# A four-layer conditioned model on one core: the first chunk of three stages normalised in the stage ahead of each, L0's last LayerNorm moved into L1's Q/K/V stage, L1's weights loaded a stage ahead

## The reference

```
L0:  res = relu(concat([x, cumulative-value attention + cond]) @ ff1 + b1) @ ff2 + b2 + x
     x = (res - mean(res)) * rsqrt(var(res) + 1e-6) * gamma + beta            # LayerNorm
L1:  h = film(rmsnorm(x, w1), cond);  Q, K, V = h @ q_w + q_b, h @ k_w + k_b, h @ v_w + v_b
     x = x + softmax(Q K^T / 16) V @ proj_w + proj_b
     h = film(rmsnorm(x, w2), cond);  x = x + gelu(h @ mlp_w1 + b1) @ mlp_w2 + b2
L2:  h = gain(cond) * layernorm(x) + shift(cond);  qkv = h @ Wqkv^T + bqkv      # 16 heads of 16
     h1 = attention(qkv) @ Wp^T + bp + x;  x = h2(h1) + h1
L3:  LayerNorm, attention with 16 heads of 64, then 8 experts on 256 tokens each
```

## Time and profile before

| | |
|---|---|
| timed runs | median 2151.21 us of 3 (2143.28 to 2153.71) |
| profiled execution | 2135.19 us, span 2133.5 us |
| mean granted TensorE clock | 0.925 |
| TensorE busy | 1863.1 us, 87% |
| VectorE busy | 1479.1 us, 69% |
| ScalarE busy | 1186.0 us, 56% |
| GpSimd busy | 817.6 us, 38% |

### The profile page before, as it was taken

One profiled execution on the slowest core, in us unless ns is written; L12 is line 12 of the kernel. 1 busy time (PEld: TensorE's weight loads), 2 busy tenths in 40 slices (PEclk: granted clock), 3 DMA queues, 4 the chain that ended last, 5 costly groups with the idle time before them and its releaser, 6 DMA issues. The chain is left out here.

```text
span 2133.5 us, 37279 instructions
## 1 busy us (share of the span) xinstructions
PE 1863.1 (87%) x14338; PEld 1188.9 (56%) x14338; DVE 1479.1 (69%) x2497; ACT 1186.0 (56%) x2034; POOL 817.6 (38%) x735
## 2 busy tenths in 40 slices
PE   5888689879879999998788969999999999984796
PEld 3665467669533333333566745555555555583686
DVE  5554644363559998992788777777777777646796
ACT  2333233232206886885456667777777777632573
POOL 4355450074121212000155654544444444304376
PEclk8999899989878998999899989999999999996698
DMA  5000100000252312112156965444554565225452
GB/s 146 1 1 0 45 8 1 31 13 1 79 153 45 95 42 46 39 45 65 65 178 204 287 161 120 113 103 104 120 120 109 123 147 136 59 85 159 135 155 48
DMA packets 196273, 191.14 MB, mean 90 GB/s; under 512 B 64192, under 2 KB 154944, under 8 KB 195840
## 3 DMA queue, kind: packets, MB, share of 16 engines
q1 hardware_dynamic: 193024, 184.56, 32.4%
q0 software_dynamic: 3072, 4.20, 1.1%
HBM read 121.07 MB, written 67.37 MB: 88 GB/s over the span
## 5 line engine op out<-in xcount | busy, mean ns | idle before, releaser
L1470 POOL TENSOR_SCALAR l3h_prob<-l3h_prob,l3h_inv 128x1024 f32<-128x1024 f32 x256 | 287.5, 1123 | 322.0 <-DVE l3h_inv L1442 322.0
L1436 DVE TENSOR_REDUCE l3h_nmax<-l3h_score 128x1 f32<-128x1024 f32 x256 | 313.5, 1224 | 139.2 <-PE l3h_score L1379 139.1
L1660 DVE TENSOR_REDUCE l2h_nm<-l2h_rowb 128x1 f32<-128x1024 f32 x256 | 302.7, 1218 | 37.4 <-PE l2h_rowb L1591 37.0
L1695 ACT ACTIVATE l2h_pT<-l2h_score 128x512 f32<-128x512 f32 x512 | 274.6, 598 | 91.4 <-PE l2h_score L1613 68.3
L1460 ACT ACTIVATE l3h_prob<-l3h_score,l3h_nmax 128x1024 f32<-128x1024 f32 x256 | 285.9, 1117 | 38.5 <-DVE l3h_nmax L1436 3.4
L1402 PE MATMUL l3h_out<-l3h_pT,l3h_vs 128*64 128x512 f32 x1024 | 274.4, 617 | 0.0
L1428 ACT ACTIVATE l3h_pT<-l3h_ring 128x512 f32<-128x512 f32 x256 | 152.8, 597 | 105.2 <-PE l3h_ring L1390 104.7
L1390 PEld LDWEIGHTS l3h_ring<-ident,l3h_prob 64*128 64x128 f32 x4096 | 172.3, 139 | 37.3 <-issue 8.0
L1426 DVE COPY l3h_pT<-l3h_ring 128x512 f32<-128x512 f32 x256 | 172.1, 672 | 2.0 <-PE l3h_ring L1390 2.0
L1390 PE MATMUL l3h_ring<-ident,l3h_prob 64*128 64x64 f32 x4096 | 169.5, 222 | 2.6 <-DVE l3h_pT L1426 2.4
L1627 PE MATMUL l2h_out<-l2h_pT,l2h_vs 128*32 128x256 f32 (+1 forms) x1792 | 162.7, 437 | 0.0
(11 more groups left out here) (449 smaller groups left out, 4346.0 us busy)
## 6 DMA issues: line engine op xcount, KB each, us to landing
q3first<-l_q SPq DMA_DIRECT2D x64, 256.0 KB, 5.0
l3h_Q<-l_q SPq DMA_DIRECT2D x64, 256.0 KB, 5.0
l_q<-l3qkv_hi SPq DMA_DIRECT2D x16, 512.0 KB, 5.1
l_q<-l3qkv_lo SPq DMA_DIRECT2D x16, 512.0 KB, 4.0
l_k<-l3qkv_hi SPq DMA_DIRECT2D x16, 512.0 KB, 3.3
l_k<-l3qkv_lo SPq DMA_DIRECT2D x16, 512.0 KB, 3.4
k3first<-l_k SPq DMA_DIRECT2D x64, 128.0 KB, 5.2
l3h_vs<-l_v SPq DMA_DIRECT2D x32, 256.0 KB, 3.1
```

The source lines that it names most:

```text
L1436: dve.tensor_reduce(self.nmax[:, t % 4:t % 4 + 1], self.score[t % 2][:, :], AX.X, ALU.max, negate=True).then_inc(self.maxes, 1)
L1470: pool.tensor_scalar(self.prob[:, q, :], self.prob[:, q, :], self.inv[:, q:q + 1], self.vscale, ALU.mult, ALU.mult).then_inc(self.scaled, 1)
L1660: dve.tensor_reduce(self.nm[:, mr % 2, at:at + 1], self.rowb[h][:, :], AX.X, ALU.max, negate=True).then_inc(self.maxes, 1)
L1695: act.activation(self.pT[:, g % 4, h, c * C:(c + 1) * C], self.score[v % 3][:, :], ACT.Exp).then_inc(self.exps, 1)
```

## The change

- **State that outlives a stage.** `CarriedNorm`, a `NormTurn` for each of the three stages, lives in a buffer `carry` (128 x 4096 numbers) and has semaphores that aren't cleared between the stages. `carry` is L0's cumulative sum, and from its last use on it holds the normalised tiles of even chunks, the statistics, L1's weights, `oT`, the first quarters of the MLP's weights and what L2 needs.
- **L0**: no LayerNorm for chunk 3; the residual is written to `X`. Behind products 2 and 3 of chunk 3 VectorE makes the statistics of chunks 0 and 1 for L1, behind product 5 it normalises chunk 0. SP loads L1's three weight matrices and a copy of gamma and beta once the cumulative sum is dead.
- **L1's Q/K/V**: VectorE starts with chunk 1's normalisation, then does L0's LayerNorm of chunk 3 (gamma and beta too), with chunk 2's statistics within it; chunk 3's statistics come behind chunk 0's copies. TensorE no longer waits for loads. L2's weights aren't loaded here.
- **Attention**: VectorE makes the statistics of chunks 0 to 2 for the MLP behind the low parts of tiles 12, 13 and 14, and normalises chunk 0 behind those of tile 15; ScalarE takes three roots behind its last high part. SP loads half of the MLP's first weight matrix.
- **MLP**: starts with chunk 1's normalisation. VectorE instead of GpSimd makes the first two low weight parts, GpSimd begins when the first input is copied, and ScalarE rounds the last four quarters ahead of GELU 3 and 4. The statistics of chunks 0 to 2 for L2 and chunk 0's normalisation are made behind group 0 of chunks 2 and 3 and before the last residual. SP loads L2's weights.
- **L2's Q/K/V**: starts with chunk 1's normalisation and chunk 3's statistics.

The core of the diff (signatures, views and semaphore lists left out):

```diff
@@ layer0: sync, scalar, vector; the pool's last finish(NC - 1) is removed
+            sp.wait_ge(clo, NC * KF)
+            for n in ("qw", "kw", "vw"):
+                sp.dma_start(g[f"l1_{n}"], w1[n].rearrange("(k p) n -> p k n", p=P)).then_inc(ahead, 16)
+            for n in ("gam", "bet"):
+                sp.dma_start(g[f"l0_{n}"], w[n].rearrange("(a n) -> a n", a=1).broadcast_to([P, D])).then_inc(ahead, 16)
+            sp.wait_ge(ahead, 16 * 5)
...
+                    if c == NC - 1 and j == 4:
+                        nt.act_root(act, 0)
+                        nt.act_root(act, 1)
...
+                    if c == NC - 1 and j in (2, 3):
+                        dve.wait_ge(shifted, (j - 1) * TC)
+                        nt.dve_stats(dve, j - 2)
+                    if c == NC - 1 and j == 5:
+                        nt.dve_norm(dve, 0)
...
+                    to = X if c == NC - 1 else res
+                if c == NC - 1:
+                    break
@@ layer1_qkv: scalar, tensor, vector
-            nt.act_start(act)
-            act.wait_ge(loaded, 96)
+            nt.act_scale(act, 0)
+            act.wait_ge(inverse0, 1)
+            act.activation(rstd[:, :], rstd[:, :], ACT.Sqrt).then_inc(root0, 1)
+            nt.act_root(act, 2)
+            act.wait_ge(loaded, 48)
...
-            pe.wait_ge(loaded, 96)
...
-            nt.dve_start(dve)
+            last = T - TC
+            nt.dve_norm(dve, 1)
+            for i in range(TC):
+                dve.bn_stats(st[:, i, :], X[:, last + i, :]).then_inc(chain0, 1)
...
             nt.dve_stats(dve, 2)
+            for i in range(TC):
+                dve.scalar_tensor_tensor(X[:, last + i, :], X[:, last + i, :], mv[:, i, 0:1], g["l0_gam"],
+                                         ALU.subtract, ALU.mult).then_inc(gained0, 1)
+            dve.wait_ge(root0, 1)
+            for i in range(TC):
+                dve.wait_ge(gained0, i + 1)
+                dve.scalar_tensor_tensor(X[:, last + i, :], X[:, last + i, :], rstd[:, i:i + 1], g["l0_bet"],
+                                         ALU.mult, ALU.add).then_inc(done0, 1)
...
+                if c == 0:
+                    dve.wait_ge(done0, TC)
+                    nt.dve_stats(dve, 3)
@@ layer1_attention: vector, scalar
                     empty(t - 1)
+                    if T - 4 < t < T:
+                        dve.wait_ge(emptied, added[t - T + 3])
+                        nt.dve_stats(dve, t - T + 3)
+                    if t == T:
+                        nt.dve_norm(dve, 0)
...
+                if t == T:
+                    for c in range(3):
+                        nt.act_root(act, c)
@@ layer1_mlp: sync, gpsimd, scalar, vector
+            sp.wait_ge(first_lo, 2)
+            for to, src in ((g["w2qkvT"], w2nd["WqkvT"]), (g["w2pT"], w2nd["WpT"])):
+                sp.dma_start(...).then_inc(kept, 16)
...
+            pool.wait_ge(xhs, KF)
             for q, (src, hi, lo) in enumerate(quarters):
+                if q < 2:
+                    continue
...
-            nt.act_root(act, 0)
             high(range(2))
-            nt.act_root(act, 1)
             nt.act_scale(act, 0)
+            nt.act_root(act, 3)
             high(range(2, 4))
-            for c in range(2, NC):
-                nt.act_root(act, c)
-            high(range(4, 8))
...
+                    if n == 2:
+                        nt.act_scale(act, 1)
+                    if n in (3, 4):
+                        high((2 * n - 2, 2 * n - 1))
...
-            nt.dve_start(dve)
+            nt.dve_norm(dve, 1)
+            for q in range(2):
+                src, hi, lo = quarters[q]
+                dve.wait_ge(whs, q + 1)
+                dve.tensor_tensor(lo, src, hi.bitcast(F32), ALU.subtract).then_inc(first_lo, 1)
+            nt.dve_stats(dve, 3)
             split(0)
-            for c in range(2, NC):
-                nt.dve_stats(dve, c)
...
+                    if c >= 2 and j == 1:
+                        dve.wait_ge(downc, (c - 1) * TC)
+                        nxt.dve_stats(dve, c - 2)
...
+            dve.wait_ge(downc, (NC - 1) * TC)
+            nxt.dve_stats(dve, 2)
+            dve.wait_ge(nt.turned, 3 * KF)
+            nxt.dve_norm(dve, 0)
             residual(NC - 1)
@@ layer2_qkv: scalar, vector
-            nt.act_start(act)
+            nt.act_scale(act, 0)
...
-            nt.dve_start(dve)
-            nt.dve_stats(dve, 2)
+            nt.dve_norm(dve, 1)
+            nt.dve_stats(dve, 3)
```

More of the change, by code:

```diff
@@ L387, in layer0 @@
         vload, cleared = s.sem("raw_values"), s.sem("rows_cleared")
+        ahead = s.sem("l1_weights")
         block = s.block()
@@ L810, in act_scale, with __init__, attach, slot @@
                            bias=self.shift[:, kf, b:b + 1], scale=self.gain[:, kf, b:b + 1]).then_inc(self.ready, 1)
-    def dve_start(self, dve):
-        for c in range(2):
-            self.dve_stats(dve, c)
-            self.dve_norm(dve, c)
-    def dve_next(self, dve, c):
-        if c + 2 < NC:
-            self.dve_norm(dve, c + 2)
-        if c + 3 < NC:
-            self.dve_stats(dve, c + 3)
-    def act_start(self, act):
-        self.act_root(act, 0)
-        self.act_root(act, 1)
-        self.act_scale(act, 0)
-    def act_next(self, act, c):
-        if c + 1 < NC:
-            self.act_scale(act, c + 1)
-        if c + 2 < NC:
-            self.act_root(act, c + 2)
     def wait_ready(self, eng, c):
         eng.wait_ge(self.ready, (c + 1) * KF)
+class CarriedNorm(NormTurn):
+    FIRST, SMALL = slice(0, TC * D), 3840
+    def __init__(self, sems, carry, X, eps, mean, name):
+        self.X, self.eps, self.mean, self.bufs, self.steps = X, eps, mean, 2, 0
+        at = self.SMALL
+        self.xnA = carry[:, self.FIRST].rearrange("p (t d) -> p t d", d=D)
+        self.st = carry[:, at:at + 6 * T].rearrange("p (t n) -> p t n", n=6)
+        self.mv = carry[:, at + 6 * T:at + 8 * T].rearrange("p (t n) -> p t n", n=2)
+        self.rstd, self.sq = carry[:, at + 8 * T:at + 9 * T], carry[:, at + 9 * T:at + 10 * T]
+        self.chain, self.inverse, self.root, self.normed, self.turned, self.ready = (sems.sem(f"{name}_{n}") for n in (
+            "chain", "inverse", "root", "normed", "turned", "ready"))
+    def attach(self, s, gain, shift, ident, banks):
+        self.gain, self.shift, self.ident, self.banks = gain, shift, ident, banks
+        self.xnB = s.sb("norm_xn", [P, TC, D])
+        self.out = s.sb("norm_out", [P, self.bufs, KF, C])
+        return self
+    def slot(self, c, t):
+        return (self.xnB if c % 2 else self.xnA)[:, t, :]
 def rows(ap):
@@ L859, in layer1_qkv @@
         bank = [s.ps(f"bank{i}") for i in range(8)]
-        nt = NormTurn(s, g["X"], g["gain"][:, 0], g["shift"][:, 0], g["ident"], bank[0:2], 1e-6, mean=False)
-        kept, loaded, scaled, qks, qkc, vs, vc, qkh, qkl, vh, vl = (s.sem(n) for n in (
-            "l2_weights", "loaded", "bias_scaled", "qk_sum", "qk_copied", "v_sum", "v_copied", "qk_hi", "qk_lo", "v_hi", "v_lo"))
+        nt = norm.attach(s, g["gain"][:, 0], g["shift"][:, 0], g["ident"], bank[0:2])
+        chain0, inverse0, root0, gained0, done0 = (s.sem(f"l0_{n}") for n in ("chain", "inverse", "root", "gained", "done"))
+        loaded, scaled, qks, qkc, vs, vc, qkh, qkl, vh, vl = (s.sem(n) for n in (
+            "loaded", "bias_scaled", "qk_sum", "qk_copied", "v_sum", "v_copied", "qk_hi", "qk_lo", "v_hi", "v_lo"))
         def qk_part(part, c, i):
@@ L989, in layer1_attention @@
             "out_copied", "inverse"))
+        ahead = s.sem("mlp_weights")
         block = s.block()
@@ L1067, in _ @@
         def _(dve):
-            use = [0]
+            use, added = [0], {}
             def empty(t):
@@ L1087, in residual @@
                     use[0] += 1
+                added[gr] = use[0]
             for t in range(T + 1):
@@ L1147, in layer1_mlp @@
         bank = [s.ps(f"bank{i}") for i in range(8)]
-        nt = NormTurn(s, X, g["gain"][:, 1], g["shift"][:, 1], g["ident"], bank[0:2], 1e-6, mean=False)
+        nt = norm.attach(s, g["gain"][:, 1], g["shift"][:, 1], g["ident"], bank[0:2])
         xbs, ups, upc, yhs, yls, downs, downc, whs, wls, xhs, xls = (s.sem(n) for n in (
@@ L1209, in _ @@
                     act.activation(y[:, n % 4, :], bank[2 + n % 4][:, :], ACT.Gelu, bias=b1[:, j:j + 1]).then_inc(upc, 1)
+            for c in range(3):
+                nxt.act_root(act, c)
         @block.tensor
```

115 lines of the change are left out of this document (70 added, 45 removed), and 3 rows, old and new, of the table views.

## The result

The change is worth 25 us or so: the median goes from 2153.71 us (13 runs, 2132.03 to 2162.03) to **2125.29 us** (13 runs, 2119.61 to 2135.21), a ratio of 0.9882 with a 95% interval of 0.9857 to 0.9906. The prediction was 2126.0. That it was met within 1 us is partly luck: the prediction subtracts 25 from a median of 2151.2, the median of all 13 runs is 2.5 higher, and the measured difference, 28.4, is larger than the forecast one by as much.

The account below looks back on a forecast made before the run. TensorE is busiest overall, but at the seams a serial chain from statistics to first real matmul was taken as the bound. Terms -17.0 - 1.6 - 6.3 = -24.9 from median 2151.2 gave 2126 us, range 2110 to 2141.

Parts of the forecast that it names:

- The sum: All three seams together: -17.0 - 1.6 - 6.3 = -24.9 us, by bounds about -31 to -16.
- Seam A: L0 to L1's Q/K/V: first projection at 222.8 instead of 239.83, -17.0 us.
- Seam C: MLP to L2's Q/K/V: first projection sooner, -6.3 us (4.5 to 7.6).
- Seam B: Attention to MLP: 4.65 gained in the MLP less 3.0 lost in attention, -1.6 us (-5 to +2.5).
- The cost, +3.0: Attention's last tiles: added statistics overrun VectorE's idle time and delay the mix, +3.0 us (+1.5 to +4.5).
- the upper bound: Attention's tail: clock falls in the longer wait, first matmuls of the mix at half clock, +4.5 us.
- Net 4.65: MLP's first chunk: turn 2 at E + 30.7 instead of E + 35.35, gaining 4.65 us before attention's cost.
- A seam doesn't move: Rival: some other wait holds the first matmul of L1 or L2, leaving about 14 of 25 (2137); chance 0.08.
- Seam B gives nothing: Rival, attention to MLP: tail costs 4.5 and the MLP's first chunk gains 4.5 at most, -20 (2131); chance 0.18.
- The two on spells at half clock: Rivals, L2's heads: spells dropped, -35 (2116), chance 0.11; or further spells at 5 us each (2161), chance 0.03.

Follow-up runs that it names:

- b1: The kernel before the change with only the two GpSimd waits in L2's heads added; 2134.07 us (7 runs), ratio 0.9911.
- p2: The changed kernel with the two GpSimd waits in L2's heads, timed in rounds; 2108.28 us (4 runs), ratio 0.9796.
- u1: The changed kernel with L0's last LayerNorm run in L0 again; 2145.99 us.
- u2: The changed kernel with L1's three Q/K/V weight matrices loaded at the start of that stage again; 2141.49 us.
- u3: The changed kernel with L2's first normalisations and statistics back in its own stage, its weights still loaded early; 2126.47 us.
- e1: The changed kernel with attention's statistics and normalisation moved from the tile loop into VectorE's wait for the mixes; 2122.91 us.
- e6: The changed kernel with attention statistics in mixes, earlier chunk-2 normalisation, later first bias additions, L2 fills behind the third normalisation, two GpSimd waits; 2095.11 us (4 runs).
- e2: The changed kernel with chunk 2's normalisation behind GELU group 2 instead of 4 in the MLP's first chunk; 2109.77 us.
- e3: The changed kernel with GpSimd's bias additions of the MLP's chunk 0 behind that chunk's low GELU parts; 2123.9 us.
- p1: The changed kernel with two more waits on GpSimd in L2's heads, delaying the 16 bias additions and the 128x2048 subtraction; 2106.54 us.

## Why the prediction was right, point by point

- **The sum**, -24.9, came out: -24.4 by the stages of all traces, 25.8 between b1 and p2, and between the medians 28.4 in the first comparison and 21.8 in the second. It came out because seams A and C, a little larger than forecast, make up for seam B.
- **Seam A, -17.0**: -17.6. First projection at 222.19, forecast 222.8; the eight LayerNorm instructions 3.3 us, forecast 3; VectorE at the first copy of Q at 228.47, forecast 228.7; the scaling held nobody. u1 and u2 show that both halves were needed. The terms as written down add up to 222.7 to 223.2 and not to 222.3 to 223.3, which changes nothing.
- **Seam C, -6.3**: -6.8, and 6.4 by u3 alone. The collision was priced from its row at 3.75 and took 4.17; the first projection comes 6.0 us behind the stage's start, forecast 5.5. From the MLP's end to that projection 5.8 were gained (12.8 to 7.0), by the stage's end 6.8; the prediction didn't have that last 1.0, and without it seam C would be below its forecast.
- **Seam B, -1.6: 0 by the ledger**, with 1.5 to either side. The cost, +3.0, came out at +3.1, but by other parts. From the first score matmul to the last mix it is 115.66 and 116.14 us without the added statistics and 117.9 in the mean of ten traces with them: the waiting grew by 2.0, not 3.0. The other 1.1 is the clock in the mix (16.54 and 19.17 to the end without, 18.97 in the mean with), which the prediction had at the upper bound only. That bound, 4.5, is met in the first pair of traces (136.49 - 132.20 = 4.3), and there only because the trace of before happened to have its last mix at full clock: b1, with the same attention as before, has 13 slow matmuls in it. Of four traces without the added statistics in the tile loop (before, b1, e1, e6) two start the mix at full clock, of ten with them none. The prediction's Trainium skill passage (TensorE: Matmul & The Clock Gate, "HAM oscillation — how this bites in real kernels") made the upper bound of this; the traces agree for the kernel with the longer wait, while before and b1, and again e1 and e6, all with the same waits of 1.83 and 1.57 us, show one mix at full clock and one at half each, so the wait alone doesn't decide. What does is open.
- **"Net 4.65" in the MLP's first chunk**: 3.1. The working took GpSimd's four low parts at 5.0 and the normalisation at 3.14 from rows of before. They took 6.15 and 4.15. The low parts now run beside VectorE's split of chunk 1 (3.48 for L1329 at 424.29), which before came later; the normalisation meets GpSimd's low GELU parts without a pause, where before there was one of 1.09 us. That this is what made them longer is argued from where they stand; no run takes it away. GELU 4 came at E + 26.9, forecast 26.3, and turn 2 at E + 32.5, forecast 30.7. The mechanism, and that turn 2 is what ends last, are shown by e2 and e3. The first product, at E + 7.8 (forecast 8.2), is 5.3 us sooner than before; turn 2, which counts, is only 2.9 sooner, and the stage 3.1.
- **The rivals.** "A seam doesn't move" fell. "Seam B gives nothing" is what the ledger says of that seam, by other amounts (3.1 lost and 3.1 gained, where the rival had 4.5 and 4.5); the forecast's -1.6 can't be told from it, in the ledger or in the time. The two on spells at half clock were right that such spells move L2's heads, and by more than the gain of seam C: the profiled execution of after lost 10.2 us there against that of before, and with the L3 stages and experts another 8, which is why its span is only 5.3 shorter. Their estimate, 4 to 6 us a spell, was too low for the changed kernel: two spells and their waits cost 19 us in the mean and 24 in the pair of after and p1, and 12.5 in the kernel before (384.3 against b1's 371.8). What they lacked was the cause, and so the cure.

## What to carry to other kernels

Work moved out of a serial seam into a neighbour's idle time gains what the chain of waits says, if each engine's queue at the new place is read too: in the MLP the same instructions took a quarter to a third longer at their new place. Where two profiled executions disagree with the medians, compare stage by stage and look for an unchanged stage that changed its length. And look for a tiny instruction with a long time: here two copies of 0.17 us that took 3.58 and 4.82 were worth 18.6 us of the changed kernel (2126.9 against 2108.3) and 14.6 of the one before (2148.7 against 2134.1), and the cure was a wait.

## What the runs showed of the hardware

- **A short VectorE copy can be held for a whole row of GpSimd instructions.** Ten traces have the copy of L2's heads meet GpSimd's 16 additions. In nine it is held 4.80 to 4.82 us, seven additions of 0.69, until the last one ends; in e2 it got in after one (0.70). In all ten the copy starts 6.25 to 6.27 us behind the first addition. Maxima beside the same additions weren't held (1.19 each). Beside the single subtraction of 128x2048 (3.62 us) all ten copies took 3.57 to 3.60. The Trainium skill (SBUF — State Buffer, "Who interferes with whom") says that a cast can contend with GpSimd, that a reduction never does, and that the first to issue keeps the shared ports for its whole instruction. The traces agree on who is held, and at the subtraction on how long; at the additions the copy was held for seven instructions, not one. Why e2's got in sooner is open.
- **What such a hold costs is mostly clock.** The copies held TensorE up by 3.5 and 4.8 us. Behind that the granted clock was at its lower level, 0.50, for about 20 and 27 us in the trace of after; over the traces it was 4 to 24 us behind the subtraction and 17 to 27 behind the additions.
- **A spell at half clock ends late though TensorE is busy.** At 730 to 750 it is busy 19.98 us of 20 at a mean clock of 0.56. The first spell of L2's heads, which begins with the stage, lasts until about 620 in e6 (39 us behind the first matmul) and until about 665 in p2 (69 us), with the same instructions. No run here tells why. It is where the heads of the traces with the two waits differ most (364.4 us in e6, 376.6 in p2).
